# Gated network formed by VectorE straight from PSUM, and subtracted maxima as one float16 row

## The chip, the cores and the metric

One core of one Trainium2 chip runs the whole program. The metric is the device time in microseconds (us) of one execution; three runs of the kernel before took 392.19, 392.0 and 389.99 us, median 392.0 us. Lower is better. The engines are TensorE (PE; its weight loads PEld), VectorE (DVE), ScalarE (ACT), GpSimd (POOL) and SyncE (SP), which here issues DMAs.

## What is computed

Two transformer layers on x of shape 8 x 256 x 128, with 16 heads of 8 features:

```
x = x + attn0(layernorm(x))        # causal, two softmaxes, gated product of both outputs
x = x + relu(layernorm(x) W1 + b1) W2 + b2
x = x + attn1(layernorm(x) with gain and offset)   # not causal, q, k, v with biases
gate = x wg;  up = x wu            # 128 -> 384, integer weights times 1/127
x = x + (silu(gate) * up) wd       # second layer's gated network, on layernorm(x)
```

The last network takes layernorm(x). silu(g) = g/2 (1 + tanh(g/2)), which is how the kernel forms it.

## The kernel before

Each layer is a run of phases, one per batch b = 0 to 7, and each phase is 16 slots s = 0 to 15, one per head. In slot s TensorE issues, in this order:

- scores(b+1, s): q k for the next batch into one of three score banks. It waits until VectorE has taken the maximum that used this bank (`maximum`, L733, one TENSOR_REDUCE per slot, with the sign turned).
- shifted(b, s): the scores again, transposed, with the maximum subtracted inside the product: rows 96 and 97 of the stack QS hold the negated maxima (a float16 high part and a float16 rest), and the same rows of KS hold ones. ScalarE takes exp of it (L554).
- in some slots pv (probabilities times v, L974), max_rows and the tails.

max_rows (L941, L942) transposes 8 heads' maxima to rows in the PSUM bank MISC[1]. It runs twice a phase: for heads 0 to 7 of the next batch in slot 10, and for heads 8 to 15 of this batch at slot M1, which is 1 in the first layer and 0 in the second. The second one needs all 16 maxima of the batch, the last of which VectorE took in slot 15 of the phase before. hi_max (ACT, L558) copies the rows to float16, lo_max (DVE, L743) forms the rest, and SP stores both rows into QS by two DMAs (L289).

The tails are what else a batch needs, one batch or two behind. In the second layer: norm_o (L749 REC, L751 Y) in slot 2, the sum with the stream on POOL (L454), variance and the root on DVE and POOL in slot 3 (L669 to L673, L365 to L373), the normalised x on ACT in slot 6 (L565), its transposes on PE in slot 9, and the gated network in slots GU = 11, 12, 13, for j = 0, 1, 2:

- PE: four matmuls (L1072) put gate and up of 128 hidden features side by side into MISC[j % 2];
- ACT: tanh of the gate half into TH (L612), then both halves scaled into SBUF, GS (L613);
- POOL: GA = TH * gate, GA = GA + gate (L464, L468), in slots 12, 13, 14;
- DVE: `hidden`, GA * up into HG, which lies in QR (L818), in slots 13 and 15 and in slot 0 of the next phase. For the last batch DVE does the POOL part as well (L813).

The down product (PE, L1082) follows in slot 3 of the next phase, and DVE adds it to the stream (L825). Every engine runs its own list strictly in the written order; semaphores join the lists.

## Time and profile before

| | |
|---|---|
| median of 3 runs | 392.0 us |
| lowest, highest | 389.99, 392.19 us |
| span of the profiled execution (first to last instruction) | 390.1 us |
| its own time beside the span | not given apart from the span |
| PE, PEld busy | 83%, 59% |
| DVE, ACT, POOL busy | 69%, 62%, 48% |

The span is divided roughly into the preparation (to 47 us), the first layer's phases (to 208 us), the passage between the layers (to 231 us), the second layer's phases (to 370 us) and the last batch's tail. A matmul record in the profile includes its pipeline, so that records overlap: one of 256 columns lasts 0.27 us in the record, and the next starts 0.11 us later. How long an engine really takes for a step is therefore read from start to start. The same holds on VectorE and ScalarE, with less overlap.

### The profile page before, as it was taken

What the parts mean: (1) busy time and instruction counts of PE and PEld (TensorE: products, weight loads), DVE (VectorE), ACT (ScalarE), POOL (GpSimd) and SP (SyncE); (2) the same over time, 40 slices, a digit from 0 to 9 for tenths busy, and PEclk for the clock granted to TensorE, in tenths of its full rate; (3) what the DMA queues carried; (4) which work ended last, traced back from release to release, by engine and by line L of the source; (5) the groups of instructions that cost most, each with busy time, mean ns of one, the idle gap of its engine ahead of it and who ended that gap; (6) DMA issues with size and microseconds to landing.
All of it is one profiled execution on the core that took longest, in us unless ns stands there. A gap on an engine that the chain in (4) does not pass through costs nothing.

```text
span 390.1 us, 9779 instructions
## 1 busy us (share of the span) xinstructions
PE 324.2 (83%) x3088; PEld 228.7 (59%) x3088; DVE 269.5 (69%) x694; ACT 242.0 (62%) x539; POOL 188.0 (48%) x475
## 2 busy tenths in 40 slices
PE   3866389889899999999878789899999999998645
PEld 2644267668676766777555457556565656665323
DVE  2999788885758676766544775787787968785123
ACT  5565627775656647565663145777869686878812
POOL 3677628794656564655673100025353442426330
PEclk9999768999999999999998869999999999999985
DMA  8565441120121212122200000110011110101000
GB/s 242 193 146 159 146 101 43 45 63 24 43 70 43 68 41 68 41 67 45 64 9 27 2 28 24 39 34 24 23 34 39 31 45 21 34 3 30 3 13 13
DMA packets 23364, 21.31 MB, mean 55 GB/s; under 512 B 3104, under 2 KB 20384, under 8 KB 23328
## 3 DMA queue, kind: packets, MB, share of 16 engines
q1 hardware_dynamic: 23328, 20.86, 19.0%
q8 instruction: 19, 0.31, 0.3%
q14 instruction: 17, 0.14, 0.1%
HBM read 13.24 MB, written 7.34 MB: 53 GB/s over the span
## 4 chain that ended last, share of the span: by engine, by line
PE 32%; DVE 21%; issue 16%; POOL 16%; ACT 7%; DMA 4%; SPq 3%; POOLq 1%; DVEq 1%; ACTq 0%
PE bank L974 6%; DVE NM L733 6%; PE bank L1023 4%; PE bank L1030 4%; POOL PB L429 3%; DVE XN L679 2%; PE bank L951 2%; POOL GA L464 2%; POOL RS L369 2%; POOL GA L468 2%; ACT PB L554 2%; DVE STAT L669 2%; DMA xs<-in_x 2%; DVE TQ L686 2%; POOL HELD L427 2%
## 5 line engine op out<-in xcount | busy, mean ns | idle before, releaser
L733 DVE TENSOR_REDUCE NM<-bank 128x3 f32<-128x384 f32 (+1 forms) x256 | 150.5, 613 | 47.5 <-PE bank L924 31.5
L554 ACT ACTIVATE PB<-bank 128x384 f32<-128x384 f32 (+1 forms) x256 | 136.0, 553 | 49.4 <-PE bank L953 27.9
L951 PE MATMUL bank<-QS,KS 128*128 128x256 f16 x256 | 71.0, 279 | 12.4 <-ACT PB L554 10.5
L974 PE MATMUL bank<-PB,VP 128*32 128x256 f32 (+1 forms) x1024 | 61.7, 358 | 7.1 <-POOL PB L429 5.6
L429 POOL TENSOR_SCALAR_AFFINE_SELECT PB<-PB 128x256 f32<-128x256 f32 x128 | 52.8, 413 | 0.0
L427 POOL TENSOR_TENSOR HELD<-EPSC 128x1 f32<-128x1 f32 x128 | 26.0, 203 | 54.5 <-ACT PB L554 53.0
L974 PEld LDWEIGHTS bank<-PB,VP 128*32 128x32 f32 x1024 | 26.7, 109 | 30.8 <-POOL PB L429 9.2
L951 PEld LDWEIGHTS bank<-QS,KS 128*128 128x128 f16 x256 | 25.0, 98 | 25.5 <-ACT PB L554 18.9
L927 PE MATMUL bank<-KS,QS 96*128 96x256 f16 x128 | 36.4, 285 | 2.3 <-issue 1.9
L464 POOL TENSOR_TENSOR GA<-TH,GS 128x256 f32<-128x256 f32 x21 | 18.2, 867 | 40.6 <-ACT GS L613 39.1
L924 PE MATMUL bank<-KS,QS 96*128 96x256 f16 x128 | 36.9, 289 | 0.0
L921 PE MATMUL bank<-MSK 128*128 128x128 bf16 x128 | 29.4, 230 | 8.5 <-DVE NM L733 8.3
L928 PE MATMUL bank<-KS,QS 96*128 96x256 f16 x128 | 36.0, 282 | 0.0
L955 PE MATMUL bank<-QS,KS 128*128 128x256 f16 x128 | 35.0, 274 | 0.0
L877 PE MATMUL bank<-IDF,XN 128*128 128x128 f32 x64 | 13.9, 302 | 19.6 <-DVE XN L679 15.8
L922 PE MATMUL bank<-KS,QS 96*128 96x128 f16 x128 | 29.6, 231 | 0.0
L923 PE MATMUL bank<-MSK 128*128 128x128 bf16 x128 | 29.3, 229 | 0.0
L953 PE MATMUL bank<-QS,KS 128*128 128x128 f16 x128 | 28.1, 220 | 0.0
L365 POOL TENSOR_TENSOR VE<-MV,EPSC 128x2 f32<-128x2 f32 x32 | 6.3, 196 | 43.4 <-DVE MV L673 43.4
L369 POOL TENSOR_TENSOR RS<-VE,EPSC 128x2 f32<-128x2 f32 x32 | 22.4, 699 | 2.5
L818 DVE TENSOR_TENSOR QR<-GA,GS 128x256 f32<-128x256 f32 x24 | 10.2, 425 | 19.0 <-POOL GA L468 18.9
L558 ACT CAST MT<-bank 8x256 f16<-8x256 f32 x32 | 11.4, 357 | 18.4 <-PE bank L942 18.4
(104 smaller groups left out, 678.2 us busy)
## 6 DMA issues: line engine op xcount, KB each, us to landing
scr<-PR SPq DMA_DIRECT2D x16, 256.0 KB, 2.3
QS<-scr SPq DMA_DIRECT2D x16, 128.0 KB, 2.7
QS<-scr SPq DMA_DIRECT2D x32, 64.0 KB, 2.8
KS<-scr SPq DMA_DIRECT2D x32, 64.0 KB, 2.7
KS<-scr SPq DMA_DIRECT2D x16, 128.0 KB, 3.0
scr<-PR SPq DMA_DIRECT2D x16, 128.0 KB, 1.9
QS<-MT SPq DMA_DIRECT2D x64, 4.0 KB
out_x<-xs SPq DMA_DIRECT2D x8, 128.0 KB, 1.9
```

The source lines that it names most:

```text
L369: pool.tensor_tensor(RS[:, n, p], VE[:, n, p], EPSC[:, 1], ALU.pow).then_inc(chain, 1)
L427: pool.tensor_tensor(HELD[:, s:s + 1], EPSC[:, 0, 0:1], EPSC[:, 0, 0:1], ALU.add)
L429: pool.affine_select(out=pr, in_=pr, compare_op=ALU.is_ge, fill=0.0, base=0, pattern=[[0, 2], [1, P]], channel_multiplier=-1).then_inc(s_c ...
L554: act.activation(PB[s % RING][:, 0:n], TB_[s % 2][:, 0:n], ACT.Exp).then_inc(s_e[L], 1)
L733: dve.tensor_reduce(NM[p][:, s, 0:n], SB_[score_bank(s)][:, 0:w].rearrange("q (n k) -> q n k", n=n), AX.X, ALU.max, negate=True).then_inc( ...
L922: pe.matmul(o[:, 0:P], q[:, 0:P], k[:, 0:P], start=False, stop=True, skip_group_check=True)
L924: ins = pe.matmul(o[:, P:3 * P], q[:, P:2 * P], k[:, :], start=False, stop=True, skip_group_check=True)
L927: pe.matmul(o[:, 0:S], q[:, 0:P], k[:, :], start=True, stop=True)
L928: ins = pe.matmul(o[:, S:2 * S], q[:, P:2 * P], k[:, :], start=True, stop=True)
L951: pe.matmul(o[:, 0:S], k[:, 0:P], q[:, :], start=True, stop=True)
L955: ins = pe.matmul(o[:, S:2 * S], k[:, P:2 * P], q[:, :], start=True, stop=True)
L974: ins = pe.matmul(o, v, pr, start=(g % 2 == 0 and kt == 0), stop=True, skip_group_check=True)
```

## The change

In the second layer's gated network ScalarE does the tanh alone, POOL nothing, and VectorE two operations per j in slot 11 + j itself: (tanh + 1) * gate, with the gate read from the PSUM bank, and that times up, read from the same bank. The scale that GS carried goes into the down weights. The banks come free when VectorE is done (`s_hg`) where ScalarE's copy freed them before (`s_gs`). In both layers the maxima are subtracted as one float16 row: lo_max and the second DMA are gone, and hi_max, now row_max, releases SP itself.

```diff
@@ -128,7 +112,7 @@
         PB = [sb(f"PB{n}", [P, 2 * S]) for n in range(RING)]
         NM = [sb(f"NM{p}", [P, H, 3]) for p in range(2)]
         NMB = [sb(f"NMB{p}", [P, H]) for p in range(2)]
-        MT = [[sb(f"MT{p}{c}", [HC, 2, S], F16) for c in range(2)] for p in range(2)]
+        MT = [[sb(f"MT{p}{c}", [HC, S], F16) for c in range(2)] for p in range(2)]
         OT = [[sb(f"OT{p}{c}", [P, S]) for c in range(2)] for p in range(2)]
         REC = [sb(f"REC{p}", [P, 16, 2]) for p in range(2)]
         Y = [sb(f"Y{p}", [P, TPB * D]) for p in range(2)]
@@ -137,7 +121,6 @@
         ZT = [sb(f"ZT{p}", [P, S]) for p in range(2)]
         HR = [TQ[p][:, :, :].rearrange("q a (b t) -> q (a b) t", t=S) for p in range(2)]
         TH = [sb(f"TH{j}", [P, S]) for j in range(NG)]
-        GS = [sb(f"GS{j}", [P, 2 * S]) for j in range(NG)]
         GA = [sb(f"GA{j}", [P, S]) for j in range(2)]
         HG = [QR[p][:, :, :, :].rearrange("q a b t -> q (a b) t")[:, 0:NG] for p in range(2)]
 
@@ -182,7 +165,6 @@
         s_mx = [sem(f"maxima_{L}") for L in range(2)]
         s_mb = sem("maxima_merged")
         s_mt = [sem(f"maxima_rows_psum_{L}") for L in range(2)]
-        s_mh = [sem(f"maxima_hi_{L}") for L in range(2)]
         s_ms = [sem(f"maxima_rows_{L}") for L in range(2)]
         s_mi = [[sem(f"maxima_in_{L}{c}") for c in range(2)] for L in range(2)]
         s_t = [sem(f"shifted_scores_{L}") for L in range(2)]
@@ -200,7 +182,7 @@
         s_h, s_hr = sem("ffn0_hidden_psum"), sem("ffn0_hidden")
         s_f = sem("ffn0_psum")
 
-        s_gu, s_gs, s_ga, s_hg = sem("gate_up_psum"), sem("gate_up"), sem("gate_part"), sem("ffn1_hidden")
+        s_gu, s_th, s_ga, s_hg = sem("gate_up_psum"), sem("gate_tanh"), sem("gate_part"), sem("ffn1_hidden")
         s_zo = sem("zero_and_one")
         s_dn = sem("ffn1_psum")
         s_xo = sem("x_final")
@@ -285,9 +267,7 @@
 
             def load_max(L, b, p, c):
                 sp.wait_ge(s_ms[L], at(2, b, c + 1))
-                for n in range(2):
-                    sp.dma_start(QS[L][p][MROW + n:MROW + n + 1, HC * c:HC * (c + 1), :],
-                                 MT[p][c][:, n, :]).then_inc(s_mi[L][c], 16)
+                sp.dma_start(QS[L][p][MROW:MROW + 1, HC * c:HC * (c + 1), :], MT[p][c][:, :]).then_inc(s_mi[L][c], 16)
 
             def store1(b, p):
                 sp.wait_ge(s_lo1, at(1, b, 1))
@@ -455,17 +435,6 @@
                                        ALU.add).then_inc(s_res[2], 1)
                 if s == 3:
                     rstd(3, c, p)
-                if s - 1 in GU and not (isinstance(c, int) and c == B - 1):
-
-                    j = GU.index(s - 1)
-                    pool.wait_ge(s_gs, at(3, c, j + 1))
-                    if j or not (isinstance(c, int) and c == 0):
-                        pool.wait_ge(s_ga, at(6, c, 2 * j))
-                    pool.tensor_tensor(GA[0][:, :], TH[j][:, :], GS[j][:, 0:S], ALU.mult).then_inc(s_ga, 1)
-                    pool.wait_ge(s_ga, at(6, c, 2 * j + 1))
-                    if j or not (isinstance(c, int) and c == 0):
-                        pool.wait_ge(s_hg, at(3, c, j))
-                    pool.tensor_tensor(GA[1][:, :], GA[0][:, :], GS[j][:, 0:S], ALU.add).then_inc(s_ga, 1)
 
             def tails(L, b, p, s):
 
@@ -553,9 +522,9 @@
                 n = 384 if L == 0 else 512
                 act.activation(PB[s % RING][:, 0:n], TB_[s % 2][:, 0:n], ACT.Exp).then_inc(s_e[L], 1)
 
-            def hi_max(L, b, p, c):
+            def row_max(L, b, p, c):
                 act.wait_ge(s_mt[L], at(2, b, c + 1))
-                act.copy(MT[p][c][:, 0], MISC[1][0:HC, 0:S]).then_inc(s_mh[L], 1)
+                act.copy(MT[p][c][:, :], MISC[1][0:HC, 0:S]).then_inc(s_ms[L], 1)
 
             def normalise(b, p):
                 act.wait_ge(s_rstd[3], at(4, b, 4))
@@ -609,8 +578,9 @@
 
                     j = GU.index(s)
                     act.wait_ge(s_gu, at(3, c, j + 1))
-                    act.activation(TH[j][:, :], MISC[j % 2][:, 0:S], ACT.Tanh, scale=0.5 * SCALE)
-                    act.mul(GS[j][:, :], MISC[j % 2][:, :], SCALE * float(np.sqrt(0.5))).then_inc(s_gs, 1)
+                    if j or not (isinstance(c, int) and c == 0):
+                        act.wait_ge(s_ga, at(3, c, j))
+                    act.activation(TH[j][:, :], MISC[j % 2][:, 0:S], ACT.Tanh, scale=0.5 * SCALE).then_inc(s_th, 1)
 
             def tails(L, b, p, s):
                 if L == 0:
@@ -623,7 +593,7 @@
                 else:
                     tail_e(b - 1, 1 - p, s)
 
-            hi_max(0, 0, 0, 0)
+            row_max(0, 0, 0, 0)
             for L in range(2):
                 if L == 1:
                     act.wait_ge(s_pv[0], 4 * B)
@@ -640,9 +610,9 @@
                         if s == 1 and later:
                             evac_o(L, b - 1, 1 - p, 1)
                         if s == M1[L]:
-                            hi_max(L, b, p, 1)
+                            row_max(L, b, p, 1)
                         if s == M0[L] and scores:
-                            hi_max(L, b + 1, 1 - p, 0)
+                            row_max(L, b + 1, 1 - p, 0)
                         if s == 11:
                             evac_o(L, b, p, 0)
                         tails(L, b, p, s)
@@ -650,7 +620,7 @@
                 evac_o(L, B - 1, 1, 1)
                 for s in range(H):
                     if L == 0 and s == M0[0]:
-                        hi_max(1, 0, 0, 0)
+                        row_max(1, 0, 0, 0)
                     tails(L, B, 0, s)
 
 
@@ -697,8 +667,8 @@
                 dve.wait_ge(s_wi, 16)
                 dve.tensor_copy(WGU[:, :], WI[:, 0:2 * HIDDEN]).then_inc(s_prep, 1)
                 dve.tensor_scalar(bqs_col, bq_col, QSCALE, None, ALU.mult).then_inc(s_prep, 1)
-                dve.tensor_scalar(WD[:, :, :], WI[:, 2 * HIDDEN:].rearrange("p (n d) -> p n d", n=NG), SCALE, None,
-                                  ALU.mult).then_inc(s_prep, 1)
+                dve.tensor_scalar(WD[:, :, :], WI[:, 2 * HIDDEN:].rearrange("p (n d) -> p n d", n=NG),
+                                  0.5 * SCALE * SCALE * SCALE, None, ALU.mult).then_inc(s_prep, 1)
                 dve.tensor_scalar(gate_row, gate_row, HADAMARD, None, ALU.mult).then_inc(s_prep, 1)
                 dve.wait_ge(s_prep, 4)
 
@@ -738,10 +708,6 @@
                     cs = slice(s + 1 - HC, s + 1)
                     dve.tensor_tensor(NMB[p][:, cs], NM[p][:, cs, 1], NM[p][:, cs, 2], ALU.min).then_inc(s_mb, 1)
 
-            def lo_max(L, b, p, c):
-                dve.wait_ge(s_mh[L], at(2, b, c + 1))
-                dve.tensor_tensor(MT[p][c][:, 1], MISC[1][0:HC, 0:S], MT[p][c][:, 0], ALU.subtract).then_inc(s_ms[L], 1)
-
             def norm_o(L, c, p):
 
                 o = MISC[0][:, :].rearrange("q (n r) -> q n r", r=32)
@@ -802,24 +768,19 @@
                 if s == 9:
                     dve.wait_ge(s_xt[3], at(1, c, 1))
                     dve.tensor_tensor(XHL[p][:, 1], MISC[1][:, 0:S], XHL[p][:, 0], ALU.subtract).then_inc(s_xlo, 1)
-                if s in (13, 15):
-                    hidden(c, p, s // 2 - 6)
+                if s in GU:
+                    hidden(c, p, GU.index(s))
 
             def hidden(c, p, j):
-                if isinstance(c, int) and c == B - 1:
-
-                    dve.wait_ge(s_gs, at(3, c, j + 1))
-                    dve.wait_ge(s_hg, at(3, c, j))
-                    dve.scalar_tensor_tensor(out=GA[1][:, :], in0=TH[j][:, :], scalar=1.0, in1=GS[j][:, 0:S],
-                                             op0=ALU.add, op1=ALU.mult).then_inc(s_ga, 1)
-                    dve.wait_ge(s_ga, at(6, c, j + 1))
-                else:
-                    dve.wait_ge(s_ga, at(6, c, 2 * j + 2))
-                dve.tensor_tensor(HG[p][:, j], GA[1][:, :], GS[j][:, S:2 * S], ALU.mult).then_inc(s_hg, 1)
+
+                dve.wait_ge(s_th, at(3, c, j + 1))
+                dve.scalar_tensor_tensor(out=GA[j % 2][:, :], in0=TH[j][:, :], scalar=1.0, in1=MISC[j % 2][:, 0:S],
+                                         op0=ALU.add, op1=ALU.mult).then_inc(s_ga, 1)
+                dve.wait_ge(s_ga, at(3, c, j + 1))
+                held()
+                dve.tensor_tensor(HG[p][:, j], GA[j % 2][:, :], MISC[j % 2][:, S:2 * S], ALU.mult).then_inc(s_hg, 1)
 
             def tail_f(c, p, s):
-                if s == 0:
-                    hidden(c, p, 2)
                 if s == 3:
                     dve.wait_ge(s_dn, at(1, c, 1))
                     dve.tensor_tensor(xt_(c), xt_(c), m1, ALU.add).then_inc(s_xo, 1)
@@ -839,8 +800,6 @@
 
             for s in range(H):
                 maximum(0, 0, 0, s)
-                if s == M0[0] + 1:
-                    lo_max(0, 0, 0, 0)
             for L in range(2):
                 def phase(b, p, scores, later):
                     for s in range(H):
@@ -852,20 +811,13 @@
 
                             cs = slice(HC * (s // 12), HC * (s // 12 + 1))
                             dve.memset(QS[1][b][:, cs].bitcast(U32), 0).then_inc(s_init[1][b], 1)
-                        if s == M1[L] + 1:
-                            lo_max(L, b, p, 1)
-                        if scores and s == M0[L] + 1:
-                            lo_max(L, b + 1, 1 - p, 0)
                         tails(L, b, p, s)
                 phases(dve, phase)
                 for s in range(H):
                     if L == 0:
                         maximum(1, 0, 0, s)
-                        if s == M0[0] + 1:
-                            lo_max(1, 0, 0, 0)
                     tails(L, B, 0, s)
-            for s in (0, 3):
-                tail_f(B - 1, 1, s)
+            tail_f(B - 1, 1, 3)
 
 
         @block.tensor
@@ -944,7 +896,7 @@
 
             def shifted(L, b, p, s):
                 if s % HC == 0:
-                    pe.wait_ge(s_mi[L][s // HC], at(32, b, 32))
+                    pe.wait_ge(s_mi[L][s // HC], at(16, b, 16))
                 if s >= 2 or not (isinstance(b, int) and b == 0):
                     pe.wait_ge(s_e[L], at(16, b, s - 1))
                 q, k, o = QS[L][p][:, s], KS[L][p][:, s], TB_[s % 2]
@@ -978,7 +930,7 @@
 
                 pe.wait_ge(s_o[L], at(2, c, 2))
                 if L == 1 and not (isinstance(c, int) and c == 0):
-                    pe.wait_ge(s_gs, at(3, c, 0))
+                    pe.wait_ge(s_hg, at(3, c, 0))
                 for t in range(TPB):
                     for k in range(2):
                         ins = pe.transpose(MISC[0][:, (2 * t + k) * P:(2 * t + k + 1) * P],
@@ -1065,7 +1017,7 @@
                     if j == 1 and free2 is not None:
                         pe.wait_ge(*free2)
                     if j == 2:
-                        pe.wait_ge(s_gs, at(3, c, 1))
+                        pe.wait_ge(s_hg, at(3, c, 1))
                     for n in range(2):
                         w = WGU[:, n * HIDDEN + j * P:n * HIDDEN + (j + 1) * P]
                         for k in range(2):
@@ -1121,8 +1073,8 @@
 
                             if L == 1 and isinstance(b, int) and b == 1:
                                 pe.wait_ge(s_va[1], B)
-                            elif L == 1 and later:
-                                pe.wait_ge(s_gs, at(3, b, -3))
+                            elif L == 1 and later and not (isinstance(b, int) and b == 1):
+                                pe.wait_ge(s_hg, at(3, b, -4))
                             elif L == 0 and with_scores:
                                 pe.wait_ge(s_mx[0], at(16, b, H + 1))
                             elif L == 0:
```

VectorE in the second layer's loop, slots 11 to 15 of the even batches' maxima and slots 0 and 1 of the next phase, the kernel before (NM is the maxima, MT the rows of maxima, QR the hidden values, GA and GS the gated parts):

```order
L733 TENSOR_REDUCE NM0<-bank2 128x2 [waits scores_1]
L743 TENSOR_TENSOR MT00<-bank7,MT00 8x256 [waits maxima_hi_1]
L733 TENSOR_REDUCE NM0<-bank0 128x2 [waits scores_1]
L733 TENSOR_REDUCE NM0<-bank1 128x2 [waits scores_1]
L818 TENSOR_TENSOR QR0<-GA1,GS0 128x256 [waits gate_part]
L733 TENSOR_REDUCE NM0<-bank2 128x2 [waits scores_1]
L733 TENSOR_REDUCE NM0<-bank1 128x2 [waits scores_1]
L818 TENSOR_TENSOR QR0<-GA1,GS1 128x256 [waits gate_part]
...
L733 TENSOR_REDUCE NM1<-bank0 128x2 [waits scores_1]
...
L818 TENSOR_TENSOR QR0<-GA1,GS2 128x256 [waits gate_part]
```

The same place after the change:

```order
L703 TENSOR_REDUCE NM0<-bank2 128x2 [waits scores_1]
L777 SCALAR_TENSOR_TENSOR GA0<-TH0,bank6 128x256 [waits gate_tanh]
L635 MEMSET HOLD 128x1 [waits gate_part]
L781 TENSOR_TENSOR QR0<-GA0,bank6 128x256
L703 TENSOR_REDUCE NM0<-bank0 128x2 [waits scores_1]
L777 SCALAR_TENSOR_TENSOR GA1<-TH1,bank7 128x256 [waits gate_tanh]
...
L703 TENSOR_REDUCE NM0<-bank1 128x2 [waits scores_1]
L777 SCALAR_TENSOR_TENSOR GA0<-TH2,bank6 128x256 [waits gate_tanh]
...
L703 TENSOR_REDUCE NM0<-bank2 128x2 [waits scores_1]
L703 TENSOR_REDUCE NM0<-bank1 128x2 [waits scores_1]
```

Before, the maxima of slots 12 and 13 stood ahead of the first hidden operation, those of 14 and 15 ahead of the second, and the third came after slot 0's. Now the first pair of operations stands ahead of slot 12's maximum, the second ahead of slot 13's, the third ahead of slot 14's, and those of slots 14 and 15 follow.

TensorE at the start of the next phase (slot 0: scores, shifted, max_rows; slot 1: scores), the kernel before:

```order
L927 MATMUL bank0<-KS11,QS11 128x256 [waits maxima_1]
L928 MATMUL bank0<-KS11,QS11 128x256
...
L951 MATMUL bank3<-QS10,KS10 128x256 [waits probs_1]
L955 MATMUL bank3<-QS10,KS10 128x256
...
L936 REGISTER_ALU [waits gate_up]
L938 ISA [waits maxima_1]
L941 MATMUL bank7<-IDF,NM0 8x128 [waits maxima_rows_1]
L942 MATMUL bank7<-IDF,NM0 8x128
L927 MATMUL bank1<-KS11,QS11 128x256 [waits maxima_1]
```

And after the change:

```order
L879 MATMUL bank0<-KS11,QS11 128x256 [waits maxima_1]
L880 MATMUL bank0<-KS11,QS11 128x256
...
L903 MATMUL bank3<-QS10,KS10 128x256 [waits probs_1]
L907 MATMUL bank3<-QS10,KS10 128x256
...
L890 ISA [waits maxima_1,ffn1_hidden]
L893 MATMUL bank7<-IDF,NM0 8x128 [waits maxima_rows_1]
L894 MATMUL bank7<-IDF,NM0 8x128
L879 MATMUL bank1<-KS11,QS11 128x256 [waits maxima_1]
```

TensorE's own order is the same; max_rows waits for the same maxima as before, and for the hidden values where it waited for ScalarE's copy.

## Rows read from the trace of the kernel before

**Rows 1.** The page: busy time of each engine.

```profile
PE 324.2 (83%) x3088; PEld 228.7 (59%) x3088; DVE 269.5 (69%) x694; ACT 242.0 (62%) x539; POOL 188.0 (48%) x475
```

**Rows 2.** Busy time by stretch, with granted clock, DMA share and GB/s.

```profile
core 0: us, PE busy (x) PEld busy (x) DVE busy (x) ACT busy (x) POOL busy (x), PEclk, DMA share, GB/s
280.00:300.00 20.00, 18.95 (x187) 12.36 (x189) 15.64 (x35) 15.90 (x38) 8.31 (x15) 1.00 0.12 30
```

**Rows 3.** Timeline of PE, second layer, max_rows and its neighbours: start, length, operation.

```profile
284.82 0.27 PE L941 MATMUL bank<-IDF,NM 128*8 128x128 f32 x1
288.21 1.60 PE L1082 MATMUL bank<-WD,QR 128*128 128x128 f32 x12
294.30 0.28 PE L951 MATMUL bank<-QS,KS 128*128 128x256 f16 x1 [0.77 <-ACT PB L554]
301.96 0.27 PE L955 MATMUL bank<-QS,KS 128*128 128x256 f16 x1
302.27 0.27 PE L941 MATMUL bank<-IDF,NM 128*8 128x128 f32 x1
```

**Rows 4.** Timeline of DVE, the same phase.

```profile
289.91 0.41 DVE L825 TENSOR_TENSOR xs<-xs,bank 128x256 f32 x1
300.52 0.42 DVE L818 TENSOR_TENSOR QR<-GA,GS 128x256 f32<-128x256 f32 x1 [0.96 <-POOL GA L468]
300.86 1.28 DVE L733 TENSOR_REDUCE NM<-bank 128x2 f32<-128x512 f32 x2
304.21 0.43 DVE L818 TENSOR_TENSOR QR<-GA,GS 128x256 f32<-128x256 f32 x1 [0.64 <-POOL GA L468]
```

**Rows 5.** Timeline of ACT and POOL, the first gated part of that phase.

```profile
297.89 0.40 ACT L612 ACTIVATE TH<-bank 128x256 f32<-128x256 f32 x1
298.17 0.62 ACT L613 ACTIVATE GS<-bank 128x512 f32<-128x512 f32 x1
...
298.95 0.73 POOL L464 TENSOR_TENSOR GA<-TH,GS 128x256 f32<-128x256 f32 x1 [5.60 <-ACT GS L613]
```

**Rows 6.** Timeline of DVE, last batch: the two operations of a pair; one that reads PSUM.

```profile
381.47 0.42 DVE L813 SCALAR_TENSOR_TENSOR GA<-TH,GS 128x256 f32<-128x256 f32 x1 [2.10 <-ACT GS L613]
381.93 0.43 DVE L818 TENSOR_TENSOR QR<-GA,GS 128x256 f32<-128x256 f32 x1
...
260.74 0.42 DVE L804 TENSOR_TENSOR XHL<-bank,XHL 128x256 f16<-128x256 f32 x1 [0.78 <-ACT XHL L607]
```

**Rows 7.** Groups of instructions, by form: the removed lo_max, and a sum read from PSUM.

```profile
L743 DVE TENSOR_TENSOR MT<-bank,MT 8x256 f16<-8x256 f32 x32 | 12.9, 402 | 1.8 <-ACT MT L558 1.7
L757 DVE TENSOR_TENSOR xs<-xs,bank 128x256 f32<-128x256 f32 x8 | 3.3, 409 | 3.6 <-PE bank L1030 3.6
```

**Rows 8.** Timeline of PE: waits for the maxima's DMA, and two pauses ahead of max_rows.

```profile
56.95 0.28 PE L951 MATMUL bank<-QS,KS 128*128 128x256 f16 x1 [0.97 <-DMA QS<-MT]
...
180.89 0.28 PE L951 MATMUL bank<-QS,KS 128*128 128x256 f16 x1 [0.62 <-DMA QS<-MT]
...
221.15 0.38 PE L941 MATMUL bank<-IDF,NM 128*8 128x128 f32 x1 [1.65 <-DVE xs L757]
250.95 0.28 PE L941 MATMUL bank<-IDF,NM 128*8 128x128 f32 x1 [1.31 <-DVE VA L792]
```

**Rows 9.** Chain that ended last, start of the first layer: start, length, what.

```profile
53.94 0.33 DVE MT L743
54.29 0.80 SPq L289
...
60.73 0.41 DVE MT L743
...
73.36 0.32 DVE MT L743
```

**Rows 10.** Timeline of PE, end of the second layer's phases.

```profile
366.86 0.61 PE L1072 MATMUL bank<-XHL,WGU 128*128 128x256 f16 x4 [0.42 <-ACT GS L613]
...
370.35 1.07 PE L974 MATMUL bank<-PB,VP 128*32 128x256 f32 x16 [1.28 <-ACT PB L554]
```


## The prediction

> **What bounds the kernel now.** The page comes first. TensorE is busiest, but no engine is busy all the time [rows 1]. In the second layer, where most of the change lies, PE is busy 18.95 of 20 us in its own records, ACT 15.90 and DVE 15.64, at full clock [rows 2]. Matmul records overlap, so the first number hides pauses. I therefore went to the chain of waits and then to the timelines of one phase.
>
> A second-layer phase lasts 302.27 - 284.82 = 17.45 us, from one max_rows in slot 0 to the next [rows 3]. Two pieces make it up.
>
> The first runs from max_rows to the first tanh. PE works in order through slots 0 to 3 to the down product, which ends at 288.21 + 1.60 = 289.81; DVE adds it at 289.91 [rows 3, 4], and the variance, the root on POOL and the normalising on ACT follow. While ACT waits for that, its exps are late and PE stands 0.77 us [rows 3]. PE then goes on to the gate matmuls in slot 11, and the tanh ends at 297.89 + 0.40 = 298.29 [rows 5]. Call this moment T. This piece is 298.29 - 284.82 = 13.47 us.
>
> The second runs from T to the next max_rows: 302.27 - 298.29 = 3.98 us. GS follows the tanh, then two POOL operations from 298.95 [rows 5]. DVE has its maxima of slots 12 and 13 behind it and stands 0.96 us for POOL before the first hidden operation at 300.52. Then come the maxima of slots 14 and 15, from 300.86 to 302.14, and 0.13 us later the transposes, which use these maxima as weights [rows 3, 4]. PE's matmul before them began at 301.96, and the next could have come 0.11 later, at 302.07. So max_rows already waits for DVE, by 0.20 us. That is the place to watch.
>
> **The change part by part.** My sum is against the profiled execution, whose span is 390.1 us; the median of the runs is 392.0, and I keep the 1.9 us between them.
>
> *VectorE from T to max_rows.* Each j now costs DVE a pair. In the last batch the kernel already runs such a pair: start to start 381.93 - 381.47 = 0.46 [rows 6]. From the second start to the next maximum is 300.86 - 300.52 = 0.34 [rows 4]. The one-element memset between the two has no row at this place; below it is 0, above 0.10, and I take 0.03, because the second operation waits for the first's result in both cases. A pair is 0.83. One maximum followed by other work takes 0.60: two end 1.28 after the first starts, and the last lasts 0.68 [rows 4]. Since the first pair stands ahead of the maximum of slot 12, all of this lies behind T: 0.04 to start, three pairs 2.49, two maxima 1.20, the last two 1.28, 0.13 to PE. The sum is 5.14, against 3.98: **+1.16 per phase**. Nothing on PE covers it: PE was free for max_rows at 302.07, T + 3.8, and even if the third gate group, which now waits for the first pair (T + 0.9), delays it by 0.3, it comes 1.0 ahead of DVE. Queued behind the waiting max_rows are slot 1, pv, slot 2's transposes and the down product, the start of the first piece.
>
> How often: phases 1 to 6 hold both gated parts and maxima, so six times. In the first piece DVE comes to L825 without its late start, but the down product ends at 289.81 and sets it anyway, so at most 0.08 comes back, in five phases. Together 6 x 1.16 - 5 x 0.08 = **+6.6**. Below: a pair of 0.80 makes +1.07 per phase. Above: with the memset at 0.10 and each of six reads of PSUM longer by 0.04, +1.6 per phase.
>
> *ScalarE without GS, POOL without GA.* ACT loses three operations of 0.62 a phase and POOL six of 0.73 [rows 5]. Neither ends the first piece, since the tanh follows slot 11's exp and comes before GS; so they are worth nothing in phases 1 to 6. In phase 7 there are no maxima. There the third gate group comes later (it ran at 366.86, after GS; now after the pair, near 367.3), but ACT is ahead by the lost copy, and the last pv, which stood 1.28 for an exp, starts some 0.3 earlier [rows 10]. In the last batch the pair reading PSUM replaces GS, and the third group waits longer by about what GS gave. **-0.3**, between -3 (the POOL part is off the path altogether) and +0.3.
>
> *lo_max and its DMA, first layer.* The steady phases there are paced by PE, ACT and their chain. A lo_max is 0.40 us, 32 times in the kernel [rows 7], yet most run beside other work: I put the steady phases at 0; above, 0.33 in each of six is 2.0. At the start it is different. PE stands 0.97 for the maxima's DMA [rows 8], and ahead of this lie lo_max 0.33 and two issues 0.80 in the chain [rows 9]; without one issue (0.40) and lo_max that is 0.7 to 0.97, I take 0.9. Three more lo_max lie in that chain, 0.41 and twice 0.32 [rows 9]: 1.05. In phase 7 of that layer PE stands 0.62 for the same DMA [rows 8]; half of it goes with the second issue, 0.35. Sum **-2.3**, between 0 (behind each stands another wait) and -4.3. The rows of maxima reach QS sooner everywhere; no other row shows PE waiting for them.
>
> Sum: 6.6 - 0.3 - 2.3 = +4.0, so a span of 394.1 and a median of **396.0**.
>
> What a read of PSUM costs VectorE is measured here. The operation that reads PSUM and writes SBUF in the same form lasts 0.42 us, the one from SBUF 0.43 [rows 6], and the sum from PSUM 0.409 [rows 7]. So reading the bank costs nothing extra in these rows, and the sum stands on that. The Trainium skill, "VectorE: DVE Perf Modes", section "Rules for kernel authors", advises copying a matmul's output to SBUF first if many operations follow, and its section on the TRN2 errata charges 62 cycles more for a PSUM source, 65 ns by its clock; by that an estimate for six reads in six phases is 2.3 us more, 398.3 in all. The trace does not agree with this charge.
>
> **The rivals.**
>
> A, *the pairs hide and the phase gets shorter*: the other side. If DVE overlaps its work so far that all three pairs and the maxima are done by the time PE reaches max_rows, the 0.20 of wait goes, and 0.08 with it: six times, -1.7, with the -0.3 and -2.3 above -4.3: 387.7. It decides at max_rows: DVE would have to need less than 3.8 us from T on. For it: POOL's stop of 0.96 is gone. Against: three pairs of even 0.5 with four maxima are 4.1. Chance 0.10.
>
> B, *the longer pause lowers TensorE's clock*. The pause before max_rows grows to 1.3, beside that of 0.77 in the same phase. A pause of 1.65 at the same place between the layers is followed by the lower level, 1.2 GHz (the record lasts 0.38), one of 1.31 in the second layer is not (0.28) [rows 8]. These two records differ by 0.10; if some 16 matmuls after max_rows (four slots of four) each take that longer, it is 1.6 us a phase, six times 9.6: 405.6. Chance 0.08, since 1.31 is the nearer row.
>
> C, *PSUM reads are slower beside PE's writes*. Between the fastest and the slowest row of 256 columns lie 0.02 to 0.04 us; at the upper end six reads are 0.24 a phase, 1.4 in all: 397.4. Chance 0.08.
>
> **How the numbers follow.** Forecast 0.74, A 0.10, B 0.08, C 0.08. The forecast's own bounds are 392 + 6.0 - 0.6 - 4.3 = 393.1 to 392 + 9.6 = 401.6 at the very ends. The range is 392 to 401: it leaves out A, B and about 0.03 of the upper end, and reaches down 1 because the runs of before themselves go to 389.99. A measurement here tells about 1%, 3.9 us, from no change. The forecast lies at that line: half of its 0.74 is above 395.9, with all of B and most of C that makes slower 0.52; the rest of it and part of A make same 0.40; A leaves faster 0.08.
>
> **What would show it.** Right: in the second layer DVE's two operations come straight after each tanh, the maximum of slot 15 ends some 5 us after the first tanh instead of 3.85, PE stands about 1.3 us before max_rows with DVE's maximum as the reason, and phases last 18.5 us; in the first layer the wait of 0.97 is gone and phases keep their length. Wrong: phases at or below 17.5 us; a pair much shorter or longer than 0.83; the tanh itself later in its phase (then the first piece is not fixed by the down product); or a first layer that shortens by more than 3 us.

## The result, and the profile after

| | before | changed |
|---|---|---|
| median of 20 runs each, same chip | 389.44 us | 391.23 us |
| lowest, highest | 386.96, 392.23 | 389.36, 394.27 |
| span of the profiled execution | 390.1 | 390.7 |
| the profiled execution's own time | not given apart | 392.38 |

The ratio is 1.0053, 95% interval 1.0029 to 1.0077: slower by 1.1 to 3.0 us. The forecast was 396.0, range 392 to 401, so the median lies below the range. Two errors add up to the 4.8 us. The kernel before reads 389.4 in twenty runs where the three shown read 392.0: 2.6 of it. The other 2.2 is the change itself, +1.8 where +4.0 was forecast.

The page of the changed kernel, busy time of the engines, and the same stretch as in [rows 2] (by stretch, with granted clock, DMA share and GB/s):

```profile
PE 319.5 (82%) x3088; PEld 228.2 (58%) x3088; DVE 268.8 (69%) x707; ACT 233.2 (60%) x515; POOL 154.4 (40%) x433
```

```profile
280.00:300.00 20.00, 18.02 (x187) 11.49 (x184) 16.34 (x43) 13.37 (x30) 2.50 (x7) 1.00 0.11 29
```

Over the program POOL is busy 34 us less than in [rows 1] and ACT 9 less, while VectorE's total stays nearly the same: most of what it lost in lo_max (12.9) it does in products. In the second layer DVE is busier, every other engine less so, and the granted clock stays full.

Where the time went can be read at one mark of each phase, the second max_rows. In the table the first three rows are the first layer's phases, the next the passage between the layers with the phases around it, then six phases of the second layer, split at T (the first tanh's end), and the end.

| stretch, us | before | changed | difference | forecast |
|---|---|---|---|---|
| start, first to second max_rows | 5.61 | 4.91 | -0.70 | -0.9 |
| phases 0 and 1 | 14.30, 15.82 | 13.32, 15.32 | -1.48 | -1.05 |
| phases 2 to 6, sum | 103.91 | 103.13 | -0.78 | 0 |
| passage | 59.13 | 59.22 | +0.09 | -0.35 |
| second layer, T to max_rows, six | 23.68 | 30.49 | +6.81 | +6.96 |
| second layer, max_rows to T, six | 79.74 | 77.50 | -2.24 | -0.4 |
| last max_rows to the end | 35.73 | 35.20 | -0.53 | -0.3 |

These sum to +1.2; the first max_rows itself came 0.57 earlier, where nothing is changed (52.18 and 51.61; over the kernels below it lies between 51.7 and 53.3), which leaves the spans 0.6 apart.

**T to max_rows.** The changed kernel's timeline of DVE (start, length, operation, and in brackets what ended the idle time before it), from the first tanh's end at 296.29:

```profile
296.33 0.42 DVE L777 SCALAR_TENSOR_TENSOR GA<-TH,bank 128x256 f32<-128x256 f32 x1 [0.71 <-ACT TH L583]
296.79 0.41 DVE L781 TENSOR_TENSOR QR<-GA,bank 128x256 f32<-128x256 f32 x1
296.81 0.06 DVE L635 MEMSET HOLD<- 128x1 f32 x1
297.12 0.68 DVE L703 TENSOR_REDUCE NM<-bank 128x2 f32<-128x512 f32 x1
297.72 0.41 DVE L777 SCALAR_TENSOR_TENSOR GA<-TH,bank 128x256 f32<-128x256 f32 x1
298.18 0.42 DVE L781 TENSOR_TENSOR QR<-GA,bank 128x256 f32<-128x256 f32 x1
...
299.90 1.88 DVE L703 TENSOR_REDUCE NM<-bank 128x2 f32<-128x512 f32 x3
```

and of PE in the same phase:

```profile
297.26 0.61 PE L1024 MATMUL bank<-XHL,WGU 128*128 128x256 f16 x4 [0.40 <-DVE QR L781]
301.42 0.27 PE L893 MATMUL bank<-IDF,NM 128*8 128x128 f32 x1 [0.96 <-DVE NM L703]
```

A pair is 0.46 and 0.33 start to start, 0.79 (forecast 0.83), the memset hides in it, and from 296.33 on DVE has no idle time. The rows left out are the second maximum, the third pair and two memsets; the last row holds the maxima of slots 14 and 15 and the next phase's first. The second of them ends at 299.90 + 1.28 = 301.18, and max_rows follows 0.24 later (forecast 0.13), 5.13 us after T; forecast were 5.14. So the sum is right to 0.01, with 0.12 less for the pairs and 0.11 more for the last step. PE waits for DVE, as said; compare [rows 3]. The third gate group stands 0.40 for the first pair, and DVE's list has no gap all the same, so that this wait ends nothing here.

**max_rows to T.** The changed kernel's PE, DVE, POOL and ACT in the phase that begins with max_rows at 283.36:

```profile
283.36 0.27 PE L893 MATMUL bank<-IDF,NM 128*8 128x128 f32 x1 [1.09 <-DVE NM L703]
...
286.61 1.50 PE L1034 MATMUL bank<-WD,QR 128*128 128x128 f32 x12
287.95 0.27 PE L879 MATMUL bank<-KS,QS 96*128 96x256 f16 x1
...
292.30 0.28 PE L903 MATMUL bank<-QS,KS 128*128 128x256 f16 x1 [0.46 <-ACT PB L523]
```

```profile
286.37 0.36 DVE L715 RECIPROCAL REC<-bank 128x32 f32<-128x32 f32 x1
...
288.15 0.42 DVE L786 TENSOR_TENSOR xs<-xs,bank 128x256 f32 x1 [0.37 <-PE bank L1034]
288.50 0.29 DVE L639 BATCH_NORM_STATS2 STAT<-xs 128x6 f32 x1
```

```profile
287.39 0.72 POOL L434 TENSOR_TENSOR xs<-xs,Y 128x256 f32 x1 [14.09 <-DVE Y L717]
```

```profile
290.89 0.88 ACT L534 ACTIVATE XN<-xs,NRS,RS 128x128 f32 x2
```

The same in the kernel before, rows that the forecast did not use:

```profile
286.73 0.42 DVE L818 TENSOR_TENSOR QR<-GA,GS 128x256 f32<-128x256 f32 x1 [0.83 <-POOL GA L468]
287.08 0.68 DVE L733 TENSOR_REDUCE NM<-bank 128x2 f32<-128x512 f32 x1
287.68 0.40 DVE L743 TENSOR_TENSOR MT<-bank,MT 8x256 f16<-8x256 f32 x1
288.01 0.67 DVE L733 TENSOR_REDUCE NM<-bank 128x2 f32<-128x512 f32 x1
288.61 0.33 DVE L749 RECIPROCAL REC<-bank 128x32 f32<-128x32 f32 x1
...
289.31 0.68 DVE L733 TENSOR_REDUCE NM<-bank 128x2 f32<-128x512 f32 x1
...
290.49 0.49 DVE L669 BATCH_NORM_STATS2 STAT<-xs 128x6 f32 x2
```

```profile
289.65 0.27 PE L927 MATMUL bank<-KS,QS 96*128 96x256 f16 x1
```

```profile
288.20 0.97 PEld L1082 LDWEIGHTS bank<-WD,QR 128*128 128x128 f32 x8 [0.25 <-issue]
```

```profile
289.60 0.72 POOL L454 TENSOR_TENSOR xs<-xs,Y 128x256 f32 x1 [2.90 <-DVE Y L751]
```

The down product writes the bank from which lo_max reads the maxima, so it cannot start before lo_max ends. And lo_max stood on DVE's list behind the third hidden operation, which waited for POOL. It ended at 288.08; the weight load began at 288.20 and the product, otherwise due at 288.07, at 288.21. That is one holder. The other is POOL's sum with the stream, over at 290.32, on which the variance at 290.49 waited, since L749 and L751 were late behind the same operations. Counted from max_rows:

| | down starts | next matmul | L825 / L786 | variance | T |
|---|---|---|---|---|---|
| before | 3.39 | 4.83 | 5.09 | 5.67 | 13.47 |
| changed | 3.25 | 4.59 | 4.79 | 5.14 | 12.93 |

In every second phase of the changed kernel the product comes 0.07 later and T is at 13.15 instead of 12.93. The gain is 0.36 to 0.57 in five phases, and what the variance gains reaches T whole. The sixth, the first of the layer, has no down product ahead and gains 0.01.

### The profile page after: what moved, and what is told of

It is laid out like the page before. It is cut to its first block, busy times and chain, and to the rows that moved or that the text cites. A ratio compares the mean times of both kernels' runs of the same rounds, so it can differ in the third digit from the quotient of the medians.

```text
span 390.7 us, 9636 instructions
## 1 busy us (share of the span) xinstructions
PE 319.5 (82%) x3088; PEld 228.2 (58%) x3088; DVE 268.8 (69%) x707; ACT 233.2 (60%) x515; POOL 154.4 (40%) x433
## 4 chain that ended last, share of the span: by engine, by line
PE 39%; DVE 22%; issue 14%; POOL 11%; ACT 7%; DMA 4%; SPq 1%; DVEq 1%; POOLq 0%; ACTq 0%
PE bank L926 9%; DVE NM L703 7%; PE bank L982 4%; PE bank L975 4%; PE bank L903 3%; POOL PB L409 3%; DVE XN L649 3%; PE bank L936 2%; DVE STAT L639 2%; POOL RS L349 2%; ACT PB L523 2%; DMA xs<-in_x 2%; DVE TQ L656 2%; PE bank L1034 2%; PE bank L879 2%
## 5 line engine op out<-in xcount | busy, mean ns | idle before, releaser
L434 POOL TENSOR_TENSOR xs<-xs,Y 128x256 f32<-128x256 f32 (+1 forms) x8 | 5.8, 726 | 107.4 <-DVE Y L717 107.4
L879 PE MATMUL bank<-KS,QS 96*128 96x256 f16 x128 | 36.1, 283 | 2.2 <-issue 1.4
L876 PE MATMUL bank<-KS,QS 96*128 96x256 f16 x128 | 36.5, 285 | 0.0
L880 PE MATMUL bank<-KS,QS 96*128 96x256 f16 x128 | 35.6, 279 | 0.0
L829 PEld LDWEIGHTS bank<-IDF,XN 128*128 128x128 f32 x64 | 8.1, 150 | 25.6 <-issue 16.9
```

The source lines that it names most:

```text
L876: ins = pe.matmul(o[:, P:3 * P], q[:, P:2 * P], k[:, :], start=False, stop=True, skip_group_check=True)
L879: pe.matmul(o[:, 0:S], q[:, 0:P], k[:, :], start=True, stop=True)
L880: ins = pe.matmul(o[:, S:2 * S], q[:, P:2 * P], k[:, :], start=True, stop=True)
```

## The experiments

Each was timed beside the kernel before on one chip (medians of 388.5 to 389.8 there). "Phases" are the second layer's, max_rows to max_rows, without the first of the six, which is shorter in every kernel (17.57 in the changed one). They come from the one profiled execution, but they repeat to 0.02 us between kernels that differ there only in operations that nobody waits for (the changed one 18.28 and 18.06, the one with the filler below 18.29 and 18.06), so they tell more than the ratio. The diffs are shortened, with ... where lines are left out.

**One row alone.** The kernel before, with one float16 row, no lo_max and one DMA; the gated network untouched.

```diff
-                for n in range(2):
-                    sp.dma_start(QS[L][p][MROW + n:MROW + n + 1, HC * c:HC * (c + 1), :],
-                                 MT[p][c][:, n, :]).then_inc(s_mi[L][c], 16)
+                sp.dma_start(QS[L][p][MROW:MROW + 1, HC * c:HC * (c + 1), :], MT[p][c][:, :]).then_inc(s_mi[L][c], 16)
...
-                        if s == M1[L] + 1:
-                            lo_max(L, b, p, 1)
```

> The kernel before with only the second part of the change: one float16 row of maxima, no lo_max, one DMA; the gated network as before. Theory 1 (two separate effects): the first layer alone gets shorter, by about 3.0 us, and in the second layer the piece from max_rows to the first tanh loses some 0.3 us in each of five phases, because the reciprocal and with it POOL's sum start earlier by the removed 0.33 us and the down product no longer waits for lo_max; the piece from the tanh to max_rows stays 3.98 us. Sum -4.5 us, ratio 0.988. Rival (the second layer's first piece got shorter only because POOL's gated part left VectorE's path): phases of the second layer keep 17.45 us, the sum is -3.0 us, ratio 0.992. Rival (the removed rows give nothing, and the first layer's shorter time in the changed kernel was chance): ratio 1.000.

Measured: 385.92 against 389.14, ratio 0.9913 (0.9878 to 0.9948). First layer as in the changed kernel (13.32, 15.32). Max_rows to T 12.96 to 13.15 in the five phases with a down product ahead, T to max_rows 3.87 to 4.09. This half of the change is a gain by itself, and the first piece shortens although POOL is as busy as before. The interval holds the expected 0.988 and the rival's 0.992 alike; what refutes the rival are the phases, 16.8 to 17.2 where the kernel before has 17.1 to 17.5. Its rows, from max_rows at 282.41:

```profile
285.66 1.50 PE L1068 MATMUL bank<-WD,QR 128*128 128x128 f32 x12
```

```profile
287.20 0.42 DVE L819 TENSOR_TENSOR xs<-xs,bank 128x256 f32 x1
287.59 0.06 DVE L663 MEMSET HOLD<- 128x1 f32 x1
287.69 0.49 DVE L667 BATCH_NORM_STATS2 STAT<-xs 128x6 f32 x2
```

```profile
286.81 0.72 POOL L452 TENSOR_TENSOR xs<-xs,Y 128x256 f32 x1 [2.58 <-DVE Y L745]
```

The product starts at 3.25, the sum at 4.79, as in the changed kernel; the variance is at 5.28 instead of 5.14, because POOL's sum still ends late, at 287.53. So of the 0.53 that the variance gained in the changed kernel, 0.39 comes with the first holder alone, and 0.14 only when POOL's part goes too.

**The gated network alone.** The changed kernel with both rows, lo_max and its DMA back.

```diff
+            def lo_max(L, b, p, c):
+                dve.wait_ge(s_mh[L], at(2, b, c + 1))
+                dve.tensor_tensor(MT[p][c][:, 1], MISC[1][0:HC, 0:S], MT[p][c][:, 0], ALU.subtract).then_inc(s_ms[L], 1)
...
```

> The changed kernel with the two float16 rows, lo_max and both DMAs put back; only the gated network is changed. Theory 1: the first layer is as in the kernel before (within 0.5 us); in the second layer the piece from the tanh to max_rows is 5.13 us instead of 3.98 in six phases, and the piece before it about 13.1 instead of 13.5, so +4.5 us, less 0.5 at the end: +4.0 us, ratio 1.010. Rival (the pairs cost little and the rest is chance of the clock): ratio 1.000 to 1.003. Rival (lo_max back in VectorE's list adds to the piece from max_rows to the tanh): above +5 us, ratio 1.013.

Measured: 392.59, ratio 1.0083 (1.0047 to 1.0119). T to max_rows 5.02 and 4.99, max_rows to T 12.91 to 13.17, the first layer's phases 0 and 1 13.96 and 15.82 (before 14.30 and 15.82). Here lo_max stands in the list with nothing late ahead of it:

```profile
284.69 0.69 DVE L706 TENSOR_REDUCE NM<-bank 128x2 f32<-128x512 f32 x1 [0.17 <-PE bank L895]
285.30 0.40 DVE L716 TENSOR_TENSOR MT<-bank,MT 8x256 f16<-8x256 f32 x1
```

It ends 1.64 after max_rows (284.06), long ahead of the product at 287.31 (3.25). Either removal clears the first holder, so their gains in this piece do not add: both alone, and both together, give about 13.

**All pairs one slot later** (slots 12, 13, 14, so behind the maxima of slots 12, 13 and 14).

```diff
-                if s in GU:
-                    hidden(c, p, GU.index(s))
+                if s - 1 in GU:
+                    hidden(c, p, GU.index(s - 1))
```

> The changed kernel with each pair of VectorE operations one slot later (slots 12, 13, 14), behind that slot's maximum. Theory 1 (it is the order of VectorE's list, not the work in it, that costs): the maximum of slot 12 fits into the 0.71 us that VectorE stands before the first pair, so one maximum less lies behind the tanh: 5.13 - 0.59 = 4.54 us from tanh to max_rows, six times, -3.5 us against the changed kernel, about -1.6 us against the kernel before, ratio 0.996. Rival (the amount of VectorE work decides, wherever it stands): no change against the changed kernel, ratio 1.005. Rival (TensorE's third gate group, which waits for the first pair, decides): also no change or slower, since the first pair cannot start earlier.

Measured: 388.31, ratio 0.9967 (0.9929 to 1.0005). T to max_rows 4.60 and 4.47, phases 17.4 to 17.8. The same work in another order is worth 0.53 a phase: one maximum fewer lies behind T.

**Pairs spread** (slots 12, 13 and 0 of the next phase, so that two stand ahead of max_rows).

```diff
-                if s in GU:
-                    hidden(c, p, GU.index(s))
+                if s in (12, 13):
+                    hidden(c, p, s - 12)
...
+                if s == 0:
+                    hidden(c, p, 2)
```

> The changed kernel with VectorE's pairs in slots 12 and 13 and the third in slot 0 of the next phase, behind the maxima that max_rows needs. The work is the same. Theory 1: behind the tanh lie two pairs and three maxima, 0.04 + 2 x 0.83 + 2 x 0.60 + 0.68 + 0.13 = 3.71 us, less than the 4.0 us that TensorE itself needs to reach max_rows, so that max_rows does not wait for VectorE any more: phases of 17.1 us instead of 18.1 to 18.3, -6.5 us against the changed kernel, about -5 us against the kernel before, ratio 0.987. Rival (amount of work decides): ratio 1.005 as the changed kernel. Rival (the third pair in slot 0 delays the reciprocal of slot 2, and gives back what the order gains): phases near 17.9, ratio 1.000.

Measured: 387.10, ratio 0.9933 (0.9903 to 0.9964). T to max_rows 4.39 and 4.25, phases 17.2 to 17.5: the expected direction, but 0.4 to 0.7 more than expected (3.71 by DVE's list, 4.0 by PE's pace), and 0.987 lies outside the interval. Its timelines show why:

```profile
295.93 0.61 PE L1027 MATMUL bank<-XHL,WGU 128*128 128x256 f16 x4 [0.47 <-DVE QR L781]
299.28 0.27 PE L896 MATMUL bank<-IDF,NM 128*8 128x128 f32 x1 [0.31 <-DVE NM L703]
```

```profile
297.18 0.68 DVE L703 TENSOR_REDUCE NM<-bank 128x2 f32<-128x512 f32 x1
298.35 1.29 DVE L703 TENSOR_REDUCE NM<-bank 128x2 f32<-128x512 f32 x2 [0.48 <-PE bank L883]
```

The third gate group needs the bank that the first pair reads; PE stands 0.47 for it, and what PE has next, the scores, comes late to DVE, which stands 0.48. A later pair holds the bank longer. That was a guess from two rows, and the next two runs test it.

**The spread order, operands in SBUF.** ScalarE copies the bank to GS again, VectorE forms both products from GS at the same three places; POOL stays out. One row.

```diff
+                    act.mul(GS[j][:, :], MISC[j % 2][:, :], SCALE * float(np.sqrt(0.5))).then_inc(s_gs, 1)
...
-                dve.scalar_tensor_tensor(out=GA[j % 2][:, :], in0=TH[j][:, :], scalar=1.0, in1=MISC[j % 2][:, 0:S],
+                dve.scalar_tensor_tensor(out=GA[1][:, :], in0=TH[j][:, :], scalar=1.0, in1=GS[j][:, 0:S],
...
-                dve.tensor_tensor(HG[p][:, j], GA[j % 2][:, :], MISC[j % 2][:, S:2 * S], ALU.mult).then_inc(s_hg, 1)
+                dve.tensor_tensor(HG[p][:, j], GA[1][:, :], GS[j][:, S:2 * S], ALU.mult).then_inc(s_hg, 1)
```

> ScalarE copies gate and up to SBUF again, VectorE forms both products from the copies, at the places of the spread version (slots 12, 13 and 0 of the next phase). Theory (the spread version lost time because the PSUM bank is held until the first pair, which delays TensorE's third gate group and with it the scores of slot 15): with the copies the third group comes on time, VectorE no longer stands 0.48 us for these scores, and from the first tanh's end to max_rows it takes: copy's end 0.54, pair 0.79, maximum 0.60, pair 0.79, maxima 0.60 and 0.68, 0.13 to PE: 4.1 us against 4.39, phases 16.9 to 17.2, ratio about 0.989. Rival (the bank is not what holds; VectorE's list alone is): the same stop stays and the wait for the copy comes on top, 4.8 us.

Measured: 387.79 against 388.51, ratio 0.9949 (0.9906 to 0.9992); the expected 0.989 lies just outside the interval. T to max_rows 4.24 and 4.10, phases 17.0 to 17.4.

```profile
296.00 0.43 DVE L795 SCALAR_TENSOR_TENSOR GA<-TH,GS 128x256 f32<-128x256 f32 x1 [0.32 <-ACT GS L600]
296.46 0.42 DVE L798 TENSOR_TENSOR QR<-GA,GS 128x256 f32<-128x256 f32 x1
...
298.20 1.88 DVE L720 TENSOR_REDUCE NM<-bank 128x2 f32<-128x512 f32 x3
```

DVE's stop of 0.48 is gone, the maxima of slots 14, 15 and 0 run without a pause, and PE does not stand before the third group; in exchange the first pair stands 0.32 for the copy. The 4.8 of the rival is refuted; 4.24 is 0.11 above the theory, which is again the last step to max_rows (0.24, from 299.48 to 299.72). Net, the bank's being held costs about 0.15 us a phase more than the copy's wait.

**The changed kernel's order, operands in SBUF** (pairs in slots 11, 12, 13; else as the last one).

```diff
-                if s in (12, 13):
-                    hidden(c, p, s - 12)
+                if s in GU:
+                    hidden(c, p, GU.index(s))
...
```

> As before it, but the pairs stand in slots 11, 12 and 13, as in the changed kernel. Only where the operands are read differs from the changed kernel in VectorE's list. Theory (the place in the list costs, the source of the operands does not): the first pair waits for the copy, until 0.54 us after the tanh; then three pairs of 0.79, two maxima of 0.60, the last two 1.28, 0.13 to PE: 5.5 us, 0.4 more than the changed kernel's 5.13; phases 18.4 to 18.7, ratio about 1.01. Rival (reading PSUM, or the bank's being held, is what made the second piece long): below 5.1 us, ratio at or below 1.00.

Measured (four executions): 395.45, ratio 1.0161 (1.0101 to 1.0221), T to max_rows 5.63 and 5.49, phases 18.4 to 18.8. Reading SBUF does not rescue this order: the source is not what made the second piece long, the place in the list is.

**Only the pair of slot 13 ahead of max_rows, operands in SBUF** (the old places of hidden: slot 13, slot 15 behind its maximum, slot 0), POOL out, one row. The diff is against the last one.

```diff
-                if s in GU:
-                    hidden(c, p, GU.index(s))
+                if s in (13, 15):
+                    hidden(c, p, s // 2 - 6)
...
+                if s == 0:
+                    hidden(c, p, 2)
```

> One float16 row, and the gated network with ScalarE's tanh and its copy GS as in the kernel before, but with VectorE forming both products from SBUF, at the old places (slots 13, 15 and 0), and POOL out of it. Theory 1 (what costs in the change is that the pairs hold the PSUM banks and stand ahead of the maxima; POOL's part was a real wait too): TensorE's third gate group waits for GS only, the maxima of slots 12 and 13 lie ahead of the first pair, and from the tanh to max_rows it takes 3.7 to 3.9 us (3.98 before, 4.08 with one row alone, 5.13 in the changed kernel); the other piece is 12.93 to 13.15 us. Six phases of 16.9 us: -3.3 us in the second layer, -3.0 in the first, about -1 at the end; -7 us against the kernel before, ratio 0.982. Rival (the amount of VectorE work in the phase decides): from the tanh to max_rows 4.5 us or more, ratio 0.995 or above. Rival (POOL's chain cost nothing, as the prediction had it for phases 1 to 6): as the kernel with one row alone, ratio 0.991.

Measured: 383.94 against 389.83, ratio 0.9858 (0.9809 to 0.9907), faster than both kernels. T to max_rows 3.85 to 3.96, phases 16.8 to 17.1. Its page by stretch, second layer, columns as above, and DVE ahead of max_rows at 295.43:

```profile
276.00:296.00 20.00, 19.04 (x195) 12.16 (x192) 16.99 (x38) 16.41 (x37) 2.50 (x7) 1.00 0.12 32
```

```profile
292.53 0.41 DVE L795 SCALAR_TENSOR_TENSOR GA<-TH,GS 128x256 f32<-128x256 f32 x1
292.98 0.42 DVE L798 TENSOR_TENSOR QR<-GA,GS 128x256 f32<-128x256 f32 x1
293.32 0.68 DVE L720 TENSOR_REDUCE NM<-bank 128x2 f32<-128x512 f32 x1
294.50 0.69 DVE L720 TENSOR_REDUCE NM<-bank 128x2 f32<-128x512 f32 x1 [0.49 <-PE bank L900]
```

DVE does as much as in the changed kernel and yet has time to spare, 0.49 us, before the last maximum.

From "one row alone" this kernel differs only in the part that POOL had, which VectorE now does. Max_rows to T is 12.94 where it took 13.08 there (13.14 in the phases between, as there), and T to max_rows 3.89 and 3.95 for 4.08. So moving POOL's part to VectorE gained about 0.15 us in the first piece of these phases and 0.13 to 0.19 in most second pieces, and the rival by which it cost nothing is refuted. The same places with the operands in PSUM were not run, so how much of the gain over the changed kernel needs the copy is not shown here; the order alone is worth more than the copy in the runs above (5.63 to 4.24 with the copy, 5.13 to 4.39 without).

**What of lo_max counted in the first layer.** Two runs: the changed kernel with an unawaited operation of lo_max's size on VectorE at each place of lo_max (first), and with a second DMA of a zero row (second).

```diff
+            def filler():
+                dve.tensor_tensor(FIL2[:, :], FILL[:, :], FILL[:, :], ALU.subtract)
...
```

> The changed kernel with a VectorE operation of lo_max's size (8 x 256, float32 in, float16 out, from SBUF) put where each lo_max stood; nobody waits for its result. It separates VectorE's time from the shorter way of the rows. Theory 1 (the first layer's gain is mostly VectorE's time: lo_max stood in the chain in phases 0 and 1 and a little in each later one): the first layer's phases 0 and 1 go back from 13.32 and 15.32 us towards 14.0 and 15.8, the later ones from 20.5 towards 20.7; the second layer stays as in the changed kernel, since there the filler falls into VectorE's pauses. Sum +1.5 to +2 us against the changed kernel, ratio to the kernel before 1.010. Rival (the gain is the earlier release of the rows and the bank, not VectorE's time): the phases stay at 13.32, 15.32 and 20.5, ratio 1.005 as the changed kernel.

```diff
+                sp.dma_start(QS[L][p][MROW + 1:MROW + 2, HC * c:HC * (c + 1), :], ZR[:, :]).then_inc(s_mi[L][c], 16)
```

> The changed kernel with a second DMA of the same size beside each DMA of the maxima, from a row of zeros into the row where the rest stood (it adds zero). It separates the DMA from lo_max. Theory 1 (the second issue costs only where TensorE waits for the rows: at the first phase of the first layer some 0.4 us, and in phase 7 of that layer another 0.35): +0.7 us against the changed kernel, ratio 1.007; the second layer's phases unchanged. Rival (the second issue on SyncE's queue delays the stacks too, in every phase): over +2 us, ratio 1.011 or more. Rival (it costs nothing): 1.005.

Measured: filler 392.88, ratio 1.0074 (1.0039 to 1.0110); phases 0 and 1 go back to 14.23 and 16.01, before's 14.30 and 15.82. Second DMA 391.56, ratio 1.0039 (1.0003 to 1.0076); phases 0 and 1 stay at 13.31 and 15.33. By the ratios neither differs from the changed kernel's 1.0053, but the phases separate them: the gain in phases 0 and 1 is VectorE's time, not the DMA's. PE's wait for a score bank in phase 0 is 1.58 with the filler and 1.00 in the changed kernel and in the one with the second DMA:

```profile
60.62 0.23 PE L889 MATMUL bank<-MSK 128*128 128x128 bf16 x1 [1.58 <-DVE NM L711]
```

```profile
59.72 0.23 PE L873 MATMUL bank<-MSK 128*128 128x128 bf16 x1 [1.00 <-DVE NM L703]
```

From the first to the second max_rows both give 5.13; kernels with one row and neither addition give 4.91 to 5.65, so the 0.7 us that was expected of the second DMA can't be told from nothing. The expectation for the later phases is not met: with the filler phases 2 to 5 take 82.31 us together, less than the changed kernel's 82.70, and not more.

## Why the prediction was wrong

**VectorE from T to max_rows: right.** 5.13 against 5.14, from durations that were all in the trace of before, each counted start to start; two terms were off by 0.1 and cancelled, which is luck: the 0.11 in the last step is seen only in kernels with one DMA of the maxima, and the forecast took its 0.13 from a kernel with two. The experiments on the order confirm the reason: three pairs and four maxima behind T 5.13, three and three 4.60, two pairs 4.39 (4.24 without the held bank), one pair 3.9 (there DVE itself waits for PE's scores).

**"At most 0.08 comes back" in the first piece: this is the step that failed.** It took the down product's start and length as given, because PE works in order and its record ended where L825 began [rows 3, 4]. But the product's own start was late. It waited for lo_max, an operation that the change removes, and lo_max waited on DVE's list behind an operation that waited for POOL, whose part the change removes as well. The forecast even said that such waits go away, and did not look at who else was waiting there. Against 0.08 the phases gave 0.36 to 0.57: 0.14 by the earlier start; 0.10 by the shorter group (its weight loads run ahead of it now, where before they began 0.01 before the product); 0.06 by DVE's list ahead of the sum; and 0.23 by POOL's sum, which had held the variance. These are the differences of the table above: 4.79 for 5.09, then 0.35 for 0.58. The first three came as well with lo_max gone and POOL's part in place (one row alone), the last in full only with POOL's part gone. In all -2.24 against -0.4, of which one row alone gives -1.88; in the phases where the changed kernel has T at 13.15 it gives the whole (13.15 too), in those with 12.93 all but 0.15 (13.08). With it fell the line that ACT's and POOL's parts "are worth nothing in phases 1 to 6": the kernel with VectorE's pairs at the old places shows about 0.15 us for POOL's part in those with 12.93. The forecast had named that possibility (-3, "the POOL part is off the path altogether"), but its sum of the lower bounds has -0.6 in that place without a reason; with the -3 the lower end would have been 390.7, and 391.2 inside.

**lo_max and its DMA in the first layer: right for phases 0 and 1, not shown for the rest.** -2.96 to the end of phase 6 against -1.95. Phases 0 and 1 gave -1.48 for -1.05, and the filler shows that this is VectorE's time. The start gave -0.70 for -0.9, but not as forecast: PE's wait of 0.97 for the DMA was to go, and it is still 0.69 in the changed kernel,

```profile
55.89 0.28 PE L903 MATMUL bank<-QS,KS 128*128 128x256 f16 x1 [0.69 <-DMA QS<-MT]
```

and up to 1.27 in others with one DMA; since such kernels take 4.91 to 5.65 for this stretch, and those with lo_max 5.20 and 5.61, the 0.70 can be chance. Phases 2 to 6 gave -0.78, put at 0. Of that 0.44 is in phase 6 alone, where kernels that are alike in the first layer differ by more (20.42 to 20.95). The other four together are -0.34, and that goes with the edit: 83.04 in both kernels with lo_max, 82.69 to 82.72 in all seven with one row alone. What makes it is open, since neither the filler nor the second DMA brings it back (82.31 and 82.30). The forecast for phase 7 is not seen: the passage is even 0.09 longer, and the wait for the DMA there, gone in the changed kernel, is 0.55 to 0.94 in five others with one DMA.

**End: -0.53 against -0.3**, its parts not separated.

**The rivals.** A (the pairs hide) did not happen; the version with one pair ahead of max_rows comes near to it, and takes 3.9 there. B (the clock falls): the pause before max_rows grew to 1.09 and 0.96, and the granted clock in this stretch stayed 1.00, so a pause of 1.1 is still without effect. The row of 1.65 that the rival leaned on doesn't bear it either. The same pause stands in the changed kernel, and the record behind it lasts 0.28; the granted clock is 1.00 from 216 to 220 us and 0.50 only from 222 to 227.

```profile
217.49 0.28 PE L893 MATMUL bank<-IDF,NM 128*8 128x128 f32 x1 [1.65 <-DVE xs L723]
```

C (PSUM reads slower beside PE's writes): all the reads from the bank shown above last 0.41 or 0.42, and the same operations from SBUF 0.41 to 0.43; start to start a pair takes 0.46 and 0.33 from PSUM, 0.46 and 0.35 from SBUF (296.00, 296.46 and the next maximum at 296.81 in the spread order).

On that last point the Trainium skill, "VectorE: DVE Perf Modes", section on the TRN2 errata, was weighed in the forecast; no row here shows its extra charge for a PSUM source. The advice to copy first, in the section "Rules for kernel authors" of the same page, turned out well in the spread order all the same (4.24 against 4.39), for another reason: the copy frees the bank. In the changed kernel's order it did not (5.63 against 5.13), since VectorE then waits for the copy. A bank that is free in time is what the Trainium skill's "Perfetto Trace Analysis", section "Matmuls", asks for, that independent groups rotate through banks so that one's evacuation overlaps the next group. The stops of 0.47 on PE with operands in PSUM, none with the copy, agree.

**The base.** Three runs of 389.99 to 392.19 were taken as a median good to under 1 us; twenty runs moved it by 2.6. The range reached 1 us below the forecast's own lower end for that; with 389.4 as the base the same sum gives 393.4, and still misses the 391.2 by 2.2.

## What to carry to other kernels

When an operation is removed, list everything that waited for it, also the writers of the buffer that it read, and everything behind it on its engine's list; a step "fixed" by one engine may itself be waiting for what goes. On a list executed in order the place of an added operation counts more than its length: put it behind the work that another engine waits for, unless it holds a bank that is needed sooner. A removal that shortens a shared wait is counted once, whichever of two causes is taken away.

## What the runs showed of the hardware

- A group of 12 matmuls (the down product) whose weight loads began with it took 1.44 us to the next matmul (kernel before); with the loads running ahead, 1.34 (changed kernel).
- The passage between the layers, with the phases around it, took between 56.0 and 59.9 us in the kernels above, with hardly an edit there; in the changed kernel its granted clock is 0.76 from 208 to 227.5. Medians that differ by 1 us can't be ordered by the span of one profile; single phases can.
- From the last maximum's end to max_rows it is 0.24 us in the kernels with one DMA of maxima, and 0.13 to 0.14 in those with two: T to max_rows is 5.02 instead of 5.13 with the gated network alone and with the second DMA, and 4.08 instead of 3.98 with one row alone. In the last two phases it is 4.99 either way. The second DMA alone brings the difference; how it does so is open.
